# Half of a second expert layer computed token-major instead of feature-major, with the orders of GpSimd and VectorE changed around it

## The chip, the cores and the metric

One core of a Trainium2 chip. The metric is the device time of one execution in microseconds (us); a kernel's time is the median over its runs.

## The reference

1024 tokens with 256 features go through two residual blocks. Block 1 is a gated unit whose weights are the context `ctx[e]` (4 experts of 256 x 256) for gate, up and down alike; each token has one expert, given by its id. Block 2 is a mixture of 16 experts of width 96, top 4 of a sigmoid router, and a shared expert.

```python
def block1(x, ids):                     # h = layernorm(x)
    e = minimum(clip(ids, 0, 12499) // 3125, 3)     # the token's expert
    z = h @ ctx[e].T
    return x + (silu(z) * z) @ ctx[e].T             # x1
def block2(x1):                         # h = layernorm(x1)
    s = sigmoid(h @ router.T)
    w = top4(s + bias) weights of s, normalised to sum 1
    routed = sum_e w[e] * (silu(h @ gate[e].T) * (h @ up[e].T)) @ down[e].T
    return x1 + routed + shared(h)
```

## The kernel before

Tokens are two halves of 512. Activations are feature-major: 128 features on the partitions, the tokens of a half along the free axis, two such chunks (KC) for 256 features. Every fp32 product is made of three fp32r matmuls (high x high, low x high, high x low), so each operand is split into a high part (ScalarE, sometimes VectorE) and a low part (GpSimd for weights, VectorE for activations). The five engines have each its own program, written out by hand in order, and meet at semaphores.

**Block 1.** A `mix(n)` is one output chunk of one layer and half, for all four experts: `mixes` numbers them (layer, half, chunk). Each expert has a PSUM bank of a ring of six (`ring_order`, `ring_bank`); `wait_ring_read` makes TensorE wait until the former contents of a bank are read. ScalarE copies expert 0 (`first_z`, semaphore `z_first`), VectorE overwrites it with experts 1 to 3 where the token's id is beyond a threshold (`pick`, `copy_predicated`, semaphore `z_picked`). For layer 1 follow silu (`silu_z`), `hidden_product`, `hidden_high` or `hidden_cast`, `hidden_low` (semaphore `h1_done`). For layer 2 `add_block_1` adds the residual `xt`, which is x feature-major and becomes x1 in place.

**The norm of block 2.** It needs token-major tiles. For half 0 TensorE transposes x1 (`x1_transposes`, line 1010) into two PSUM banks during mix 5; VectorE takes the statistics there (`tile_stats`, L670; `layer_norm_vars`, L676 and L678), GpSimd the power -0.5 (`rstd_of`, L478), VectorE and ScalarE normalise two tiles each (L721, L542), and TensorE turns the tiles back (`norm_transposes`, L987) for the high and low parts xn_hi, xn_lo (`x_high`, `x_low`; semaphores `xhi_done`, `xlo_done`). Half 1 goes through DRAM instead (`turn_x1`, `write_x1`, `read_x1`, `turn_xn`, `write_xn`, `read_xn`), during the items of block 2.

**Block 2.** Item g is a pair (half, chunk of 128 hidden columns); chunk 0 is the shared expert with the router's logits. `gate_or_up(g)` are the products, `product`, `hidden_2`, `hid_high` and `hid_low` make the hidden chunk, `down(g)` follows two items later. The router's part of VectorE is `turn_logits` (L796, L800), `mark_best` (L807 to L816) and `normalise_scores` (L821 to L833); the combine rows go to DRAM and come back spread over partitions (`write_rows`, `spread_rows`) on the queue of SyncE (SP). `output(h)` adds `xt`.

**Weights.** 15 pieces are loaded by SP into four stage slots in order, `load_piece(n)` waiting for the high and the low part of piece n-4 (`w_hi`, `w_lo`). `high_part` is ScalarE's, `low_part` GpSimd's (L468 in one call, L472 in two calls of 512). Pieces 0 to 3 are ctx, 4 the shared expert and router, 5 and 8, 9, ... gate and up, 6 the shared down weights, 7, 10, 13 the down weights.

## Time and profile before

| | us |
|---|---|
| median of 3 runs (169.2 to 170.2) | 169.52 |
| the profiled execution | 169.34 |
| its span, first to last instruction | 167.2 |
| TensorE busy | 162.5 |
| VectorE / ScalarE / GpSimd busy | 114.5 / 68.7 / 37.2 |

The profile is of one execution. PE is TensorE's matmuls, PEld its weight loads, DVE VectorE, ACT ScalarE, POOL GpSimd, SPq the issues on SyncE's queue. Times in the trace are microseconds from the span's start. L1030 is line 1030 of the kernel before.

### The profile page before, as it was taken

Reading aid. Unit: us, or ns where it says so; the run is one execution under the profiler, and the core shown is the slowest. Engines: PE = TensorE matmul, PEld = TensorE weight load, DVE = VectorE, ACT = ScalarE, POOL = GpSimd, SP = SyncE. Lnnn points to the kernel's source line nnn. Section 1 sums busy time; section 2 is a strip of 40 time slices with the busy share of each in tenths; the row PEclk is TensorE's granted clock in tenths of the full one; section 3 lists DMA queues with packets and bytes.
Section 4 is the critical chain, followed back from the end, with each engine's and each line's share of the span. In section 5 each row is a group of like instructions: output and inputs, shape, how many; then the busy total and the mean of one; then the engine's idle time right before and its main releaser. Section 6 shows DMA issues by size and latency. Waiting matters only on the chain.

```text
span 167.2 us, 2186 instructions
## 1 busy us (share of the span) xinstructions
PE 162.5 (97%) x705; PEld 128.9 (77%) x705; DVE 114.5 (68%) x237; ACT 68.7 (41%) x116; POOL 37.2 (22%) x36
## 2 busy tenths in 40 slices
PE   7999999999999999999999999999999999999992
PEld 2788888888778888888888878888888888888880
DVE  1889999666957998779986744967714444444462
ACT  3654342831359134536734538452222222222210
POOL 1384000656241045556970000000000000000000
PEclk9999999999999999999999999999999999999999
DMA  5891380164304065987225400025441112200003
GB/s 172 275 408 44 107 291 0 21 206 161 115 4 127 16 205 192 219 240 211 67 61 163 153 0 4 1 103 165 173 141 67 63 63 63 65 0 0 4 0 125
DMA packets 12199, 18.78 MB, mean 112 GB/s; under 512 B 3772, under 2 KB 6044, under 8 KB 12060
## 3 DMA queue, kind: packets, MB, share of 16 engines
q1 hardware_dynamic: 12188, 18.64, 34.9%
q8 instruction: 6, 0.10, 0.2%
q14 instruction: 5, 0.04, 0.1%
HBM read 16.39 MB, written 2.24 MB: 111 GB/s over the span
## 4 chain that ended last, share of the span: by engine, by line
PE 95%; DMA 2%; DVE 1%; DVEq 0%; issue 0%
PE bank L1030 23%; PE bank L1131 15%; PE bank L1129 13%; PE bank L1130 13%; PE bank L1149 7%; PE bank L1152 7%; PE bank L1150 7%; DMA first<-first_d 2%; PE bank L998 1%; PE bank L1071 1%; PE bank L1065 1%; PE bank L1126 1%; PE bank L1125 1%; PE bank L987 1%; PE bank L1078 1%; PE bank L1060 1%
## 5 line engine op out<-in xcount | busy, mean ns | idle before, releaser
L1131 PE MATMUL bank<-xn_lo,gu_hi 128*128 128x512 f32 (+1 forms) x104 | 41.1, 395 | 0.0
L1129 PE MATMUL bank<-xn_hi,gu_lo 128*128 128x512 f32 x96 | 38.0, 396 | 0.0
L1130 PE MATMUL bank<-xn_hi,gu_hi 128*128 128x512 f32 x96 | 38.0, 396 | 0.0
L599 ACT ACTIVATE h_hi<-hid 128x512 fp32r<-128x512 f32 (+1 forms) x26 | 16.4, 632 | 45.6 <-DVE hid L860 45.6
L865 DVE TENSOR_TENSOR h_lo<-hid,h_hi 128x512 fp32r<-128x512 f32 (+1 forms) x26 | 18.0, 691 | 14.9 <-ACT h_hi L599 14.9
L1131 PEld LDWEIGHTS bank<-xn_lo,gu_hi 128*128 128x128 f32 (+1 forms) x104 | 19.4, 187 | 4.9
L589 ACT ACTIVATE act_sb<-bank 128x512 f32<-128x512 f32 (+1 forms) x26 | 15.4, 592 | 17.5 <-PE bank L1131 17.4
L472 POOL TENSOR_TENSOR gu_lo<-stage,gu_hi 128x512 fp32r<-128x512 f32 x12 | 17.2, 1457 | 21.7 <-ACT gu_hi L504 16.3
L1129 PEld LDWEIGHTS bank<-xn_hi,gu_lo 128*128 128x128 f32 x96 | 18.0, 188 | 4.4
L1130 PEld LDWEIGHTS bank<-xn_hi,gu_hi 128*128 128x128 f32 x96 | 18.0, 188 | 4.3
L749 DVE COPY_PREDICATED prod<-beyond,bank 128x512 f32<-128x512 uint8 x24 | 17.6, 737 | 5.1 <-PE bank L1030 4.4
L1149 PE MATMUL bank<-h_hi,wd_lo 128*128 128x512 f32 (+1 forms) x52 | 20.6, 396 | 0.0
L1150 PE MATMUL bank<-h_hi,wd_hi 128*128 128x512 f32 (+1 forms) x52 | 20.6, 395 | 0.0
L1152 PE MATMUL bank<-h_lo,wd_hi 128*128 128x512 f32 (+1 forms) x52 | 20.5, 395 | 0.0
L860 DVE TENSOR_TENSOR hid<-prod,bank 128x512 f32<-128x512 f32 x24 | 16.5, 688 | 2.0
L847 DVE TENSOR_TENSOR prod<-act_sb,ids 128x512 f32<-128x512 f32 x12 | 9.6, 796 | 8.6 <-ACT act_sb L589 8.6
L847 DVE TENSOR_TENSOR prod<-act_sb,first 128x512 f32<-128x512 f32 x12 | 10.0, 832 | 6.3 <-ACT act_sb L589 5.7
L1030 PE MATMUL bank<-h_hi,ctx_hi 128*128 128x512 f32 x32 | 12.7, 398 | 0.0
L1030 PE MATMUL bank<-h_lo,ctx_hi 128*128 128x512 f32 x32 | 12.7, 395 | 0.0
L1030 PE MATMUL bank<-h_hi,ctx_lo 128*128 128x512 f32 x32 | 12.7, 395 | 0.0
L1152 PEld LDWEIGHTS bank<-h_lo,wd_hi 128*128 128x128 f32 (+1 forms) x52 | 9.8, 188 | 2.4
L1150 PEld LDWEIGHTS bank<-h_hi,wd_hi 128*128 128x128 f32 (+1 forms) x52 | 9.8, 188 | 2.3
(102 smaller groups left out, 213.2 us busy)
## 6 DMA issues: line engine op xcount, KB each, us to landing
stage<-gu_d SPq DMA_DIRECT2D x6, 512.0 KB, 3.9
stage<-wd_d SPq DMA_DIRECT2D x3, 512.0 KB, 4.3
first<-comb_d SPq DMA_DIRECT2D x8, 192.0 KB, 2.9
ids<-comb_d SPq DMA_DIRECT2D x8, 192.0 KB, 3.3
stage<-ctx_d SPq DMA_DIRECT2D x4, 256.0 KB, 6.0
xt<-xt_d SPq DMA_DIRECT2D x1, 1024.0 KB, 9.9
first<-comb_d SPq DMA_DIRECT2D x8, 128.0 KB, 3.0
ids<-comb_d SPq DMA_DIRECT2D x8, 128.0 KB, 2.9
```

The source lines that it names most:

```text
L472: ins = nc.gpsimd.tensor_tensor(lo[:, s], st[:, s], hi[:, s].bitcast(F32), ALU.subtract)
L749: nc.vector.copy_predicated(prod[:, n % 2], beyond[:, e - 1, h * HALF:(h + 1) * HALF], ring_bank("z", n, e)[:]).then_inc(z_picked, 1)
L847: nc.vector.tensor_tensor(prod[:, g % 2], act_sb[:, g % 2], rows, ALU.mult).then_inc(prod_done, 1)
L860: nc.vector.tensor_tensor(hid[0:w, g % 2], src, up_bank(g)[0:w, :], ALU.mult).then_inc(hid_done, 1)
L865: nc.vector.tensor_tensor(h_lo[0:w, slot[g]], hid[0:w, g % 2], h_hi[0:w, slot[g]].bitcast(F32), ALU.subtract).then_inc(hlo_done, 1)
L1030: return nc.tensor.matmul(ring_bank("z", n, e)[:], (ctx_hi, ctx_lo)[a][:, m, e, k], parts[k][b], start=start, stop=stop)
L1129: nc.tensor.matmul(out[:], gu_lo[:, cols], xn_hi[:, h, k], start=(k == 0), stop=False)
L1130: nc.tensor.matmul(out[:], gu_hi[:, cols], xn_hi[:, h, k], start=False, stop=False)
L1131: ins = nc.tensor.matmul(out[0:rows, :], gu_hi[:, wide], xn_lo[:, h, k], start=False, stop=(k == KC - 1))
L1149: nc.tensor.matmul(acc[k][:], wd_lo[0:w, c, cols], hi, start=(c == 0), stop=False)
L1150: nc.tensor.matmul(acc[k][:], wd_hi[0:w, c, cols], hi, start=False, stop=False)
L1152: ins = nc.tensor.matmul(acc[k][:], wd_hi[0:w, c, cols], lo, start=False, stop=(c == ITEMS - 1))
```

## The change

Layer 2 of block 1 for half 0 is computed token-major by `row_mix`: a tile of 128 tokens of the hidden state is the stationary operand, and the columns of two experts (2 x 256) are the moving one, so a bank holds two experts for one tile. ScalarE copies expert 0 (`row_z`), VectorE picks experts 1 to 3 with a mask per partition (`pick_rows`) and adds x (`add_rows`); x1 is then token-major in `x1_rows`, where the statistics and the normalisation read it. The transposes of x1 of half 0 go. The tokens of a tile are permuted (`hidden`), and the turn of the normalised tiles undoes this. The output of half 0 still needs x1 feature-major: VectorE turns it in blocks of 32 (`turn_x0`, items 8 and 9) and it goes through DRAM (`write_x0`, `read_x0`, items 12 and 13) into `xt`. `xt` of half 0 holds x token-major until then, loaded by a DMA of its own; the ids come a second time, one per partition and tile.

Mix (1, 1, 1) now comes after `row_mix`, so there are 6 mixes. GpSimd takes `rstd_of(0)` ahead of piece 2 and `rstd_of(1)` ahead of piece 3; `rstd_of(2)` and the wait for xn_lo of half 0 come ahead of pieces 6 and 7 (before, behind them). VectorE does all picks of mix 3 ahead of `layer_norm_apply(2)`; before, the statistics came between the first pick and the other two of that mix.

```diff
...
-        ring_order = [("z", n, e) for n in range(7) for e in range(E1)]
-        ring_order += [("gate", 0, 0), ("up", 0, 0)] + [("z", 7, e) for e in range(E1)]
+            count = (HALVES * KC if what == "n2" else 0) + h * KC + k + 1
+            eng.wait_ge(xhi_done, max(count, KC))
+            eng.wait_ge(xlo_done, count)
+
+        ring_order = [("z", n, e) for n in range(3) for e in range(E1)]
+        ring_order += [("rows", t, pair) for t in range(TT) for pair in range(2)]
+        ring_order += [("z", n, e) for n in (3, 4) for e in range(E1)]
...
+            elif what == "rows" and e == 0:
+                eng.wait_ge(row_first, n + 1)
+                eng.wait_ge(row_picked, n * (E1 - 1) + 1)
+            elif what == "rows":
+                eng.wait_ge(row_picked, (n + 1) * (E1 - 1))
         def side_bank(what, h, c):
...
+        def hidden(tile, b, at):
+
+            if b >= KC:
+                return tile[:, at]
+            order = "p (b t j) -> p b t j" if tile is hid else "p (t b j) -> p b t j"
+            return tile[:, at].rearrange(order, t=TT, j=LANES)
         def widths(c):
...
-            sp.dma_start(xt[:], xt_d).then_inc(xt_in, 16)
+            sp.dma_start(xt[:, :, HALF:], xt_d[:, :, HALF:]).then_inc(xt_in, 16)
+            sp.dma_start(id_rows[:], id_rows_d).then_inc(id_rows_in, 16)
+            sp.dma_start(xt[:, :, 0:HALF], x_rows_d).then_inc(x_rows_in, 16)
             sp.dma_start(bias[:], bias_d.partition_broadcast(P)).then_inc(bias_in, 16)
...
+
+            def write_x0():
+                sp.wait_ge(x0_turned, TT)
+                rows = turn_d.rearrange("q k i (b c) -> b i (q k) c", c=P)
+                blocks = x[:, TT:].rearrange("p t d -> p (t d)").rearrange("p (m c) -> p m c", c=P)
+                for b in range(QUARTERS):
+                    sp.dma_start(rows[b], blocks[b * LANES:(b + 1) * LANES]).then_inc(x0_out, 16)
+
+            def read_x0():
+                sp.wait_ge(x0_out, QUARTERS * 16)
+                rows = turn_d.rearrange("q k i n -> q i k n")
+                for q in range(QUARTERS):
+                    sp.dma_start(xt[q * LANES:(q + 1) * LANES, :, 0:HALF], rows[q]).then_inc(x0_back, 16)
...
             pool.wait_ge(deviation_zero, 1)
-            for n in range(E1):
+            low_part(0)
+            low_part(1)
+            rstd_of(0)
+            low_part(2)
+            rstd_of(1)
+            low_part(3)
+            for n in range(E1, E1 + 2):
                 low_part(n)
-            rstd_of(0)
-            rstd_of(1)
-            for n in range(E1, E1 + 3):
-                low_part(n)
-            pool.wait_ge(x1_done, KC)
-            low_part(E1 + 3)
             rstd_of(2)
             pool.wait_ge(xlo_done, (HALVES + 1) * KC)
-            for n in range(E1 + 4, early_pieces + 4):
+            for n in range(E1 + 2, early_pieces + 4):
                 low_part(n)
             rstd_of(3)
...
             first_z(2)
-            first_z(3)
+            row_z(0)
             silu_z(2)
             hidden_high(2)
+            row_z(1)
             high_part(4)
             high_part(5)
+            row_z(2)
             high_part(6)
-            first_z(4)
+            row_z(3)
             high_part(7)
             high_part(8)
             router_low_rows()
-            first_z(5)
-            silu_z(5)
+            first_z(3)
+            silu_z(3)
             apply_norm(2)
             x_high("n2", 0, 0)
             x_high("n2", 0, 1)
-            first_z(6)
+            first_z(4)
             router_logits(0)
             score(0)
             silu_gate(0)
-            first_z(7)
+            first_z(5)
             hid_high(0)
             late_pieces = {1: 9, 2: 10, 3: 11, 5: 12, 6: 13, 7: 14}
...
+
+            def pick_rows(t, experts=range(1, E1)):
+
+                dve.wait_ge(row_first, t + 1)
+                dve.wait_ge(rows_masked, E1 - 1)
+                for e in experts:
+                    dve.wait_ge(row_done, 2 * t + e // 2 + 1)
+                    if e > 1:
+                        dve.wait_ge(row_picked, t * (E1 - 1) + e - 1)
+                    z = ring_bank("rows", t, e // 2)[:, e % 2 * D:(e % 2 + 1) * D]
+                    nc.vector.copy_predicated(x1_rows[:, t], beyond_rows[:, e - 1, t:t + 1].to_broadcast([P, D]),
+                                              z).then_inc(row_picked, 1)
+
+            def add_rows(t):
+
+                dve.wait_ge(row_picked, (t + 1) * (E1 - 1))
+                dve.wait_ge(x_rows_in, 16)
+                residual = xt[:, t * D // HALF, t * D % HALF:][:, 0:D]
+                nc.vector.tensor_tensor(x1_rows[:, t], x1_rows[:, t], residual, ALU.add).then_inc(row_added, 1)
+
+            def turn_x0(first):
+
+                dve.wait_ge(xn_out, QUARTERS * 16)
+                blocks = x[:, TT:].rearrange("p t d -> p (t d)").rearrange("p (q k t i) -> p t k q i", k=KC, t=TT, i=LANES)
+                for t in range(first, first + 2):
+                    for k in range(KC):
+                        ins = nc.vector.transpose(blocks[:, t, k],
+                                                  x1_rows[:, t, k * P:(k + 1) * P].rearrange("p (q i) -> p q i", i=LANES))
+                    ins.then_inc(x0_turned, 1)
+
             def hidden_product(n):
...
             masked.append(thresholds(1))
+            row_thresholds()
             pick(2, masked[1])
-            pick(3, masked[0], [1])
+            pick_rows(0, [1])
             hidden_product(2)
-            pick(3, masked[0], [2])
+            pick_rows(0, [2])
             hidden_low(2)
-            pick(3, masked[0], [3])
-            add_block_1(3)
-            pick(4, masked[0])
+            pick_rows(0, [3])
+            add_rows(0)
+            for t in range(1, TT):
+                tile_stats(2, t - 1)
+                pick_rows(t)
+                add_rows(t)
+            tile_stats(2, TT - 1)
+            layer_norm_vars(2)
+            pick(3, masked[1])
+            layer_norm_apply(2)
+            hidden_product(3)
+            hidden_cast(3)
+            hidden_low(3)
+            x_low("n2", 0, 0)
+            x_low("n2", 0, 1)
+            pick(4, masked[1], [1])
+            turn_logits(0)
+            pick(4, masked[1], [2])
+            normalise_scores(0, mark_best(0))
+            pick(4, masked[1], [3])
             add_block_1(4)
             pick(5, masked[1], [1])
-            for t in range(TT):
-                tile_stats(2, t)
-            layer_norm_vars(2)
+            hidden_2(0)
             pick(5, masked[1], [2, 3])
-            layer_norm_apply(2)
-            hidden_product(5)
-            hidden_cast(5)
-            hidden_low(5)
-            x_low("n2", 0, 0)
-            x_low("n2", 0, 1)
-            pick(6, masked[1], [1])
-            turn_logits(0)
-            pick(6, masked[1], [2])
-            normalise_scores(0, mark_best(0))
-            pick(6, masked[1], [3])
-            add_block_1(6)
-            pick(7, masked[1], [1])
-            hidden_2(0)
-            pick(7, masked[1], [2, 3])
-            add_block_1(7)
+            add_block_1(5)
             hid_low(0)
             for g in range(1, N):
...
-                ins.then_inc(side_done, 1)
+            def row_mix():
+
+                hi, lo = ([w[:, b].rearrange("p (t c) -> p t c", c=P) for b in range(KC)] for w in (h_hi, h_lo))
+
+                def moving(w, pair, k):
+                    return w[:, :, 2 * pair:2 * pair + 2, k].rearrange("p m e f -> p e m f")
+
+                for t in range(TT):
+                    for pair in range(2):
+                        wait_ring_read(pe, "rows", t, pair)
+                        out = ring_bank("rows", t, pair)[:].rearrange("p (e m f) -> p e m f", e=2, m=KC)
+                        for k in range(KC):
+                            if t == 0 and pair == 0:
+                                pe.wait_ge(h1_high, k + 1)
+                            nc.tensor.matmul(out, hi[k][:, t], moving(ctx_hi, pair, k), start=(k == 0), stop=False)
+                            nc.tensor.matmul(out, hi[k][:, t], moving(ctx_lo, pair, k), start=False, stop=False)
+                            if t == 0 and pair == 0:
+                                pe.wait_ge(h1_done, k + 1)
+                            ins = nc.tensor.matmul(out, lo[k][:, t], moving(ctx_hi, pair, k), start=False, stop=(k == KC - 1))
+                        ins.then_inc(row_done, 1)
             def mix(n, between={}, experts=range(E1), features=range(KC)):
...
             first_mix()
             mix(1, {1: lambda: norm_transposes("n1", 1, 1)})
-            for n in range(2, 5):
-                mix(n)
-            mix(5, {1: lambda: (x1_transposes(0, 0), x1_transposes(0, 1))})
-            mix(6, features=[0])
+            mix(2)
+            row_mix()
+            mix(3)
+            mix(4, features=[0])
             norm_transposes("n2", 2, 0)
-            mix(6, experts=[0, 1], features=[1])
+            mix(4, experts=[0, 1], features=[1])
             gate_or_up(0, False)
             gate_or_up(0, True)
-            mix(6, experts=[2, 3], features=[1])
-            mix(7)
+            mix(4, experts=[2, 3], features=[1])
+            mix(5)
             for g in range(1, N):
                 gate_or_up(g, False)
```

## Rows read from the trace of the kernel before

**Rows 1.** The page: busy time by engine, PE's busy slices, the chain.

```profile
PE 162.5 (97%) x705; PEld 128.9 (77%) x705; DVE 114.5 (68%) x237; ACT 68.7 (41%) x116; POOL 37.2 (22%) x36
...
PE   7999999999999999999999999999999999999992
...
PE 95%; DMA 2%; DVE 1%; DVEq 0%; issue 0%
```

**Rows 2.** The chain in order of time: start, duration, what.

```profile
39.06 0.87 PE bank L1010 x8
```

**Rows 3.** Timeline of VectorE, 14 to 47 us: start, duration, instruction, idle before.

```profile
14.67 0.73 DVE L721 TENSOR_SCALAR xn<-first,meanvar,rstd 128x256 f32<-128x256 f32 x2
...
28.69 0.69 DVE L757 TENSOR_TENSOR hid<-act_sb,prod 128x512 f32<-128x512 f32 x1
...
39.83 1.41 DVE L670 BATCH_NORM_STATS2 stats<-bank 128x6 f32<-128x256 f32 x4
...
42.77 0.74 DVE L749 COPY_PREDICATED prod<-beyond,bank 128x512 f32<-128x512 uint8 x1 [0.16 <-PE bank L1030]
...
43.46 0.99 DVE L721 TENSOR_SCALAR xn<-bank,meanvar,rstd 128x256 f32<-128x256 f32 x2
...
45.55 0.69 DVE L769 TENSOR_TENSOR h_lo<-hid,h_hi 128x512 fp32r<-128x512 f32 x1
```

**Rows 4.** Timeline of TensorE, 46 to 57 us.

```profile
46.72 0.39 PE L1030 MATMUL bank<-h_lo,ctx_hi 128*128 128x512 f32 x1
...
56.01 0.40 PE L1030 MATMUL bank<-h_hi,ctx_hi 128*128 128x512 f32 x1
```

**Rows 5.** Timeline of GpSimd, 34 to 64 us.

```profile
34.79 0.74 POOL L468 TENSOR_TENSOR wd_lo<-stage,wd_hi 96x256 fp32r<-96x256 f32 x1
37.91 2.54 POOL L472 TENSOR_TENSOR wd_lo<-stage,wd_hi 128x512 fp32r<-128x512 f32 x2 [2.38 <-DVE xt L777]
41.94 1.01 POOL L478 TENSOR_TENSOR rstd<-vareps,power 128x4 f32<-128x4 f32 x1 [1.49 <-DVE vareps L678]
48.33 2.55 POOL L472 TENSOR_TENSOR gu_lo<-stage,gu_hi 128x512 fp32r<-128x512 f32 x2 [5.38 <-DVE xn_lo L728]
60.63 2.99 POOL L472 TENSOR_TENSOR gu_lo<-stage,gu_hi 128x512 fp32r<-128x512 f32 x2 [9.75 <-ACT gu_hi L504]
```

**Rows 6.** Timeline of VectorE, 50 to 56 us: logits, top-4, picks.

```profile
50.73 0.24 DVE L800 TENSOR_TENSOR logit<-turned 128x64 f32<-128x64 f32 x1
51.48 0.74 DVE L749 COPY_PREDICATED prod<-beyond,bank 128x512 f32<-128x512 uint8 x1 [0.51 <-PE bank L1030]
52.11 0.21 DVE L807 TENSOR_TENSOR biased<-scores,bias 128x64 f32<-128x64 f32 x1
52.35 0.41 DVE L811 MAX8 best<-biased 128x8 f32<-128x16 f32 x4
...
53.66 0.23 DVE L821 SCALAR_TENSOR_TENSOR weight<-marked,scores 128x64 f32<-128x64 f32 x1
...
55.09 0.70 DVE L749 COPY_PREDICATED prod<-beyond,bank 128x512 f32<-128x512 uint8 x1
```

**Rows 7.** Timeline of VectorE where GpSimd is or isn't at work.

```profile
9.46 0.65 DVE L678 TENSOR_SCALAR vareps<-meanvar 128x4 f32<-128x4 f32 x1
...
12.50 0.17 DVE L678 TENSOR_SCALAR vareps<-meanvar 128x4 f32<-128x4 f32 x1
...
60.86 1.61 DVE L847 TENSOR_TENSOR prod<-act_sb,first 128x512 f32<-128x512 f32 x1 [0.18 <-DMA first<-comb_d]
```

**Rows 8.** Timeline of GpSimd and TensorE, 8 to 14 us.

```profile
8.79 3.80 POOL L468 TENSOR_TENSOR ctx_lo<-stage,ctx_hi 128x512 fp32r<-128x512 f32 x3 [1.01 <-ACT ctx_hi L504]
12.55 1.18 POOL L478 TENSOR_TENSOR deviation<-vareps,power 128x4 f32<-128x4 f32 x1
...
12.84 0.40 PE L1030 MATMUL bank<-xn_hi,ctx_hi 128*128 128x512 f32 x1
```

**Rows 9.** Timeline of VectorE and TensorE, 94 to 99 us.

```profile
94.66 1.28 DVE L728 TENSOR_TENSOR xn_lo<-xn,xn_hi 128x512 fp32r<-128x512 f32 x2
...
98.46 0.40 PE L1131 MATMUL bank<-xn_lo,gu_hi 128*128 128x512 f32 x1
```

More of the change, by code:

```diff
@@ L62 @@
 XN_TURN, XN_WRITE, XN_READ = 6, 10, 11
+X0_TURN, X0_WRITE, X0_READ = 8, 12, 13
 SPREADS = 4
@@ L201, in wait_side_read @@
             what, h, k, _ = before[-1]
-            if what in ("n1", "n2"):
-                count = (HALVES * KC if what == "n2" else 0) + h * KC + k + 1
-                eng.wait_ge(xhi_done, max(count, KC))
-                eng.wait_ge(xlo_done, count)
-            else:
-                eng.wait_ge(normed_v, (HALVES + 1) * TT // 2)
-                eng.wait_ge(normed_a, (HALVES + 1) * TT // 2)
-        ring_order = [("z", n, e) for n in range(7) for e in range(E1)]
-        ring_order += [("gate", 0, 0), ("up", 0, 0)] + [("z", 7, e) for e in range(E1)]
+            count = (HALVES * KC if what == "n2" else 0) + h * KC + k + 1
[4 more added lines that the diff above has]
+        ring_order += [("z", n, e) for n in (3, 4) for e in range(E1)]
+        ring_order += [("gate", 0, 0), ("up", 0, 0)] + [("z", 5, e) for e in range(E1)]
         ring_at = {u: n for n, u in enumerate(ring_order)}
@@ L296, in wait_mixed @@
             layer, h, m = mixes[n]
-            eng.wait_ge(h1_done if layer == 1 else x1_done, h * KC + m + 1)
+            if layer == 1:
+                eng.wait_ge(h1_done, h * KC + m + 1)
+            else:
+                eng.wait_ge(x1_done, m + 1)
         downs = [place[h, c] for h in range(HALVES) for c in range(ITEMS)]
@@ L450, in _ @@
                     read_xn()
+                if g == X0_WRITE:
+                    write_x0()
+                if g == X0_READ:
+                    read_x0()
                 if g == place[1, SPREADS]:
@@ L523, in first_z, with row_z @@
                 nc.scalar.activation(prod[:, n % 2], ring_bank("z", n, 0)[:], ACT.Copy).then_inc(z_first, 1)
+            def row_z(t):
+                act.wait_ge(row_done, 2 * t + 1)
+                nc.scalar.activation(x1_rows[:, t], ring_bank("rows", t, 0)[:, 0:D], ACT.Copy).then_inc(row_first, 1)
             def centre(t):
@@ L546, in hidden_high @@
                 act.wait_ge(h1_product, b + 1)
-                nc.scalar.activation(h_hi[:, b], hid[:, b % 2], ACT.Copy).then_inc(h1_high, 1)
+                nc.scalar.activation(hidden(h_hi, b, b), hidden(hid, b, b % 2), ACT.Copy).then_inc(h1_high, 1)
             def router_low_rows():
@@ L750, in pick, with row_thresholds @@
                                               ring_bank("z", n, e)[:]).then_inc(z_picked, 1)
+            def row_thresholds():
+                dve.wait_ge(id_rows_in, 16)
+                for e in range(1, E1):
+                    nc.vector.tensor_scalar(beyond_rows[:, e - 1], id_rows[:], float(e * PER_EXPERT), None,
+                                            ALU.is_ge).then_inc(rows_masked, 1)
+            def pick_rows(t, experts=range(1, E1)):
[21 more added lines that the diff above has]
+                    ins.then_inc(x0_turned, 1)
             def hidden_product(n):
@@ L762, in hidden_cast @@
                 dve.wait_ge(h1_product, b + 1)
-                nc.vector.tensor_scalar(h_hi[:, b], hid[:, b % 2], 1.0, None, ALU.mult).then_inc(h1_high, 1)
+                nc.vector.tensor_scalar(hidden(h_hi, b, b), hidden(hid, b, b % 2), 1.0, None, ALU.mult).then_inc(h1_high, 1)
             def hidden_low(n):
@@ L768, in hidden_low @@
                 dve.wait_ge(h1_high, b + 1)
-                nc.vector.tensor_tensor(h_lo[:, b], hid[:, b % 2], h_hi[:, b].bitcast(F32),
+                nc.vector.tensor_tensor(hidden(h_lo, b, b), hidden(hid, b, b % 2), hidden(h_hi, b, b).bitcast(F32),
                                         ALU.subtract).then_inc(h1_done, 1)
```

51 lines of the change are left out of this document (30 added, 21 removed).

## The prediction

> **What bounds the kernel now.** I read the page first. TensorE (PE) is busy for 97% of the span, and the chain that ended last is 95% PE [rows 1]; its busy row stands at 9 tenths or more in every slice but the first and the last [rows 1]. So the time is the length of PE's own program plus the moments in which it waits, and between those two slices it waits nowhere. An edit can help only by what it takes off PE, and hurts as soon as another engine comes later than PE's next need. The second view is therefore the timeline of PE around the edit, and the third those of VectorE (DVE) and GpSimd (POOL), to find how long ahead of PE each product is ready.
>
> **What it takes off PE.** The second layer of half 0 keeps its arithmetic: two `mix` calls of 4 experts x 2 chunks x 3 products are 48 matmuls of 512 columns; `row_mix` has 4 tiles x 2 expert pairs x 2 chunks x 3 = 48 of 512 columns too. Only the stationary and the moving side change places. Eight transposes of x1 go, and the chain has them as one piece of 0.87 us [rows 2]. PE starts a 512-column matmul each 0.233 us (162.5 us of busy time for 705, a few of them small [rows 1]), so 0.87 us is everything that the edit can give: 0.51% of the span. The moving side is now four runs of 128 elements with gaps, and no row shows such a read; I take it at nothing, as the transposes and half-width matmuls go at the pace of their columns. The other bound would be half speed, 48 x 0.233 = 11 us slower; nothing in the trace speaks for it.
>
> **The row picks (31 to 44 us).** Two copies, six picks and two adds of 512 columns become four copies (ScalarE), twelve picks and four adds of 256. A 512-wide pick takes 0.74 us [rows 3]. A 256-wide operation on PSUM takes 0.50 (the two normalisations take 0.99) and 0.35 to 0.41 per statistics call (1.41 for four) [rows 3]; so a pick lies between 0.37 (half) and 0.74 (no saving), and I take 0.47. A tile then costs DVE 3 x 0.47 + 0.42 for the add + 0.37 for the statistics = 2.2 us, and PE delivers a tile each 12 x 0.233 = 2.8 us. DVE starts behind, since half 1's hidden product comes between. The last pick of mix 2 ends some 0.7 before the hidden product, which starts at 28.69 [rows 3]; with three new 128x4 thresholds I put it at 28.2. From there DVE has 12 picks 5.6, 4 adds 1.7, 4 statistics 1.5, product and low part 1.4, aggregation and epsilon 0.6, then three 512-wide picks of mix 3 at 0.75 = 2.25: 13.0 us, plus about 0.6 waiting for ScalarE: 41.8. The third pick can't start before PE has finished mix 3: it started at 42.77, so 41.9 now, and would end at 42.65, against 43.51 before [rows 3]: hidden. But each add reads two SBUF tensors, and POOL's low parts of pieces 4 and 5, which follow ScalarE's high parts behind the hidden product, run then; as below, an add that meets one waits for it. Two such waits of 0.7 to 0.9 put the end at 43.4. What still hides that: the two vector normalisations read SBUF now (0.73 a pair at 14.67, instead of 0.99), and the low part of the hidden product ends at 46.24 before, while PE's third matmul of the next group, which reads it, starts at 46.72 [rows 3, 4]. Limit for the pick's end: (46.72 - 0.87) - (46.24 - 43.51 - 0.26) = 43.38. So 0 to 0.2 us are lost here. With picks at 0.74 it would be 12 x 0.27 = 3.2 more.
>
> **The two weight pieces (46 to 56 us), the decisive part.** Before, POOL has done pieces 6 and 7 by 40.45, and after half 0's xn_lo it has only piece 8, two calls, 48.33 to 50.88, with DVE's logits and top-4 behind it [rows 5, 6]. Now rstd_of(2) goes first and pieces 6, 7 and 8 all follow xlo_done: from 48.33 - 0.87 = 47.46, 0.74 for piece 6 and twice 2.55: to 53.3 at least [rows 5]. That gains nothing where it is meant to, since the norm waits for DVE's third pick (42.65), not for the power (1.0 us from about 41.2, so 42.3 [rows 5]). And it collides. When DVE has an operation whose operands lie in SBUF while POOL works, it waits for the end of POOL's call: the epsilon add took 0.65 us at 9.46, ending with POOL's second ctx piece, and 0.17 at 12.50; the product at 60.86 took 1.61 instead of 0.69, with POOL's pair at 60.63 stretched to 2.99 [rows 5, 7, 8]. Statistics and picks from PSUM show no such growth.
> Times, all shifted by 0.87. The logit sum (50.73 before) comes at 49.86, inside piece 7's second call (49.47 to 50.73), and ends near 50.9. The third mix's pick then runs to 51.6 and the bias add (52.11 before, 51.24 shifted) meets piece 8's first call (50.9 to 52.15): the top-4 chain begins at 52.4 instead of 51.48 [rows 6]. That is 0.92 late. Its max and match calls have one SBUF tensor and should pass; the next with two, the weight product (53.66 before, 53.7 now), comes just when piece 8's second call ends (52.35 to 53.6). So rows and the last pick are 0.92 late: the pick ends at 55.79 - 0.87 + 0.92 = 55.84. PE needs just that pick: expert 3 of the last mix overwrites the bank that it reads. Before, it ended at 55.79 and PE's matmul started at 56.01 [rows 4, 6]; now PE is there at 55.14. It waits until about 55.9: 0.77 us lost. A loss upstream isn't added, since POOL's start doesn't move with it.
> The Trainium skill, in "SBUF — State Buffer", section "SBUF: two separate sides", says that a DVE operation with two SBUF inputs or in a two-port mode and a GpSimd operation hold one port pair in turn, each for the whole instruction. The trace agrees (0.65 against 0.17, 1.61 against 0.69). By it the match calls, with a single SBUF input, are free.
>
> **The first 25 us.** The power for half 0 now comes ahead of ctx piece 2 and that for half 1 ahead of piece 3. Piece 1 ends at 10.06; 1.0 to 1.2 for the power and 1.27 for piece 2 give 12.5, and mix 1 starts at 12.84 [rows 8]: 0.3 of cover. Piece 3 ends at 15.0 and makes the shift and the normalisations of half 1 0.3 late; its PE consumers stand 0.05 to 0.5 behind. The deviations turn after the thresholds either way. I take 0, bounds 0 and +0.3.
>
> **Transfers and the way back.** xt becomes two loads of half the size and a third of 2 KB for the ids, issued in the first microseconds and needed from 31 us; hidden, though the small rstd rows queue behind them as they do now. SP's load of piece 12 waits for piece 8's low part (53.6) and stands ahead of the combine rows, which come just before the last pick (55.1): no cost. At g = 8 and 9 DVE gets 8 block transposes of 128x128, about 0.3 each, 1.2 per item. The second set delays half 1's xn_lo from 94.66 to about 96.4; its first piece (0.65) is done at 97.1 and PE reads it at 98.46 [rows 9]: 1.3 us spare. The four writes hold SP until x0 is turned, then spread rows and read back are done by 103, and `output(0)` comes at 117. All 0.
>
> **Sum.** Profiled execution 169.34 (span 167.2 + 2.1). 169.34 - 0.87 + 0.77 = 169.24, that is -0.1; on the median of 169.52 it is 169.4. A difference of 0.5%, 0.85 us, is about what a measurement can tell.
>
> **Rivals.** (a) *Full gain*, 168.65 to 169.0: the logit sum or the bias add slips between two POOL calls. For it: 0.3 us of misalignment decides each. Against: POOL works without a gap from 47.5 to 53.5. Chance 0.22; only its lowest third is over 0.5% faster. (b) *Slower*: the top-4 chain is held a second time, by piece 8's second call, because the match calls need the port after all or because the weight product comes before 53.6. Price: another 1.27, on the median 169.52 - 0.87 + 0.77 + 1.27 = 170.7. It decides when POOL's last call ends later than 53.7 and holds DVE for over 0.95. For it: the margin of 0.1. Against: the statistics calls pass freely. Chance 0.13. (c) *Row chain late*: picks near 0.74 put 1 to 3 us before PE at 45 us: 169.5 + 0.3 to 172. Chance 0.08, half of it over 0.5%. (d) The forecast, 169.1 to 169.8: 0.57.
>
> Range 168.6 (nothing lost) to 170.5. Faster by over 0.5%: 0.08; within: 0.76; slower: 0.16.
>
> **What the profile after would show.** 697 matmul records instead of 705; no transposes of xt; `row_mix` with 48 matmuls at 0.233 without a gap; picks of 256 at 0.4 to 0.5; POOL busy from 47.5 to 53.5; the logit sum and the bias add at 0.8 and 0.6 us instead of 0.24 and 0.21; one PE gap of some 0.7 us before the last mix's fourth expert, released by DVE's pick. No gap there is (a); a match or weight call of over 1 us is (b); a PE gap near 45 us is (c). Wrong altogether if `row_mix` matmuls last longer than 0.40.

## The result, and the profile after

The kernel became slower. Six executions of it take 171.43 us in the median (171.19 to 171.91), six of the kernel before on the same chip 169.86 (169.2 to 170.2); the ratio is 1.0112, with an interval of 1.0095 to 1.013. The forecast was 169.4 and its range ended at 170.5. The profiled execution took 171.42 us with a span of 169.3, where the one before took 169.34 with 167.2.

The page of the kernel after, the lines that answer to [rows 1]:

```profile
PE 161.9 (96%) x697; PEld 127.3 (75%) x697; DVE 122.0 (72%) x256; ACT 69.1 (41%) x118; POOL 37.0 (22%) x36
...
PE   7799999999999599999999999999999999999992
...
PEclk9999999999999999999999999999999999999999
...
PE 88%; DVE 3%; DMA 3%; issue 2%; ACT 1%; POOL 1%; SPq 0%; DVEq 0%; POOLq 0%
```

TensorE has 0.6 us less to do and eight matmuls fewer, as it should. But one slice in the middle, the fourteenth, falls to 5 tenths, and the second is down from 9 to 7. The view of TensorE's waits names what ended each (columns: us in total, times, longest). The wait of 1.2 us stands in the kernel before too; the two last are for the first `ctx` pieces:

```profile
PE bank L1132 <- DVE prod L798: 1.9, 1, 1.9
PE bank L1067 <- DVE warm L961: 1.2, 1, 1.2
PE bank L1180 <- ACT ctx_hi L541: 0.9, 1, 0.9
PE bank L1167 <- POOL ctx_lo L505: 0.2, 1, 0.2
```

The first is the wait for VectorE's pick before the last mix's expert 3, the very one that the prediction named. The timeline of TensorE shows its size; it answers to [rows 4]:

```profile
55.71 0.40 PE L1132 MATMUL bank<-h_lo,ctx_hi 128*128 128x512 f32 x1
57.99 0.49 PE L1132 MATMUL bank<-h_hi,ctx_hi 128*128 128x512 f32 x1 [1.89 <-DVE prod L798]
```

From start to start that is 2.28 us, where 0.23 is the pace: 2.05 lost. The timelines of VectorE and GpSimd show why, against [rows 6] and [rows 5]. VectorE:

```profile
50.60 3.15 DVE L885 TENSOR_TENSOR logit<-turned 128x64 f32<-128x64 f32 x1
53.66 0.72 DVE L798 COPY_PREDICATED prod<-beyond,bank 128x512 f32<-128x512 uint8 x1
54.29 0.20 DVE L892 TENSOR_TENSOR biased<-scores,bias 128x64 f32<-128x64 f32 x1
...
57.26 0.68 DVE L798 COPY_PREDICATED prod<-beyond,bank 128x512 f32<-128x512 uint8 x1
```

GpSimd:

```profile
47.92 0.74 POOL L505 TENSOR_TENSOR wd_lo<-stage,wd_hi 96x256 fp32r<-96x256 f32 x1 [5.36 <-DVE xn_lo L777]
48.62 2.54 POOL L509 TENSOR_TENSOR wd_lo<-stage,wd_hi 128x512 fp32r<-128x512 f32 x2
51.11 2.55 POOL L509 TENSOR_TENSOR gu_lo<-stage,gu_hi 128x512 fp32r<-128x512 f32 x2
```

The logit sum, 0.24 us of work, took 3.15. It reached VectorE at 50.60, half a microsecond before piece 7's second call ended, and did not run when that ended at about 51.1, nor at the boundary at about 52.4, but only when GpSimd's whole run was over at 53.66. Everything behind it, the last pick at 57.26 instead of 55.09 before, is 2.2 us late.

The whole difference of 2.1 us in span adds up by the first starts of the stages of TensorE. Before and after, with what each stage adds in brackets, they are: half 0's second layer 24.90 and 25.35 (+0.45), the transposes of the norm behind it 45.37 and 44.94 (-0.88, the removed transposes), the gate of half 0 47.64 and 47.51 (+0.30), expert 3 of the last mix 56.01 and 57.99 (+2.11, the gap of 2.05 and its surroundings). The +0.45 comes with the waits for the first `ctx` pieces in the list above, which vary by the execution (see experiment 1). Without it +1.6 would be left, which is also the difference of the medians. That agreement is in part chance: the profiled execution before is 0.5 us under its median, and whether the other executions after have the +0.45 isn't known.

### The profile page after: what moved, and what is told of

It reads as the page before. It is cut to its first block, busy times and chain, and to the rows that moved or that the text cites. A ratio compares the mean times of both kernels' runs of the same rounds, so it can differ in the third digit from the quotient of the medians.

```text
span 169.3 us, 2206 instructions
## 1 busy us (share of the span) xinstructions
PE 161.9 (96%) x697; PEld 127.3 (75%) x697; DVE 122.0 (72%) x256; ACT 69.1 (41%) x118; POOL 37.0 (22%) x36
## 4 chain that ended last, share of the span: by engine, by line
PE 88%; DVE 3%; DMA 3%; issue 2%; ACT 1%; POOL 1%; SPq 0%; DVEq 0%; POOLq 0%
PE bank L1233 14%; PE bank L1132 14%; PE bank L1232 13%; PE bank L1231 13%; PE bank L1251 7%; PE bank L1254 7%; PE bank L1252 7%; DMA stage<-ctx_d 3%; PE bank L1109 2%; PE bank L1113 2%; PE bank L1110 2%; PE bank L1167 1%; PE bank L1173 1%; PE bank L1080 1%; DVE prod L798 1%
## 5 line engine op out<-in xcount | busy, mean ns | idle before, releaser
L798 DVE COPY_PREDICATED prod<-beyond,bank 128x512 f32<-128x512 uint8 x18 | 13.1, 735 | 0.6
L1251 PEld LDWEIGHTS bank<-h_hi,wd_lo 128*128 128x128 f32 (+1 forms) x52 | 9.8, 188 | 2.4
L1132 PE MATMUL bank<-xn_hi,ctx_hi 128*128 128x512 f32 x24 | 9.6, 399 | 0.0
L1132 PE MATMUL bank<-xn_lo,ctx_hi 128*128 128x512 f32 x24 | 9.5, 395 | 0.0
```

The costliest lines, as they stand in the source:

```text
L1132: return nc.tensor.matmul(ring_bank("z", n, e)[:], (ctx_hi, ctx_lo)[a][:, m, e, k], parts[k][b], start=start, stop=stop)
L1251: nc.tensor.matmul(acc[k][:], wd_lo[0:w, c, cols], hi, start=(c == 0), stop=False)
```

## The experiments

Each kernel ran beside the kernel before on the same chip; that one's median was 169.3 to 169.6 in all of them. "Run" below means a row of GpSimd calls that follow one another at once.

**1. Undo one part: the two weight pieces stay ahead of the power.**

```diff
-            for n in range(E1, E1 + 2):
+            for n in range(E1, E1 + 4):
                 low_part(n)
             rstd_of(2)
             pool.wait_ge(xlo_done, (HALVES + 1) * KC)
-            for n in range(E1 + 2, early_pieces + 4):
+            for n in range(E1 + 4, early_pieces + 4):
```

> The changed kernel with GpSimd's low parts of pieces 6 and 7 back ahead of rstd_of(2). Theory A (the logit sum is held by GpSimd's unbroken run over pieces 6, 7 and 8, 50.60 to 53.75): the sum takes 0.25 us again, the PE gap of 2.1 us before the last mix's fourth expert is gone, and the time is that of before minus 0.87 plus what is lost elsewhere (0.45 early, 0.3 at the hidden low part at most): 168.9 to 169.8, ratio to before 0.995 to 1.000. Rival B (the row picks and the new waits make VectorE late whatever GpSimd does): it stays at 171.4, ratio 1.01.

Measured: 169.15 us (168.73 to 170.23, 12 executions), ratio 0.9982 (0.9963 to 1.0002). The gap in the last mix is gone. The timeline of VectorE at the logits:

```profile
50.79 0.23 DVE L885 TENSOR_TENSOR logit<-turned 128x64 f32<-128x64 f32 x1
```

So the moved pieces cost the time, and the rest of the change gives at most a few tenths.

Where the +0.45 of the kernel after comes from is only in part clear. ScalarE's first high part of `ctx` started at 5.75 us before, 6.40 after, and 5.72 to 5.97 in all experiments but 15. Experiments 11, 14 and 15 profile one kernel three times: the high part starts at 5.75, 5.72 and 6.84, the second layer at 24.69, 24.86 and 25.80, and only the last has waits for `ctx` (0.8 and 0.2). So a late `ctx` is of the execution and can cost 1 us. But this experiment has `ctx` on time (5.88) and its second layer starts at 25.22, little ahead of 25.35; how much of the +0.45 the late `ctx` made isn't shown.

Of the 0.87, then, 0.32 is lost here by the start of the second layer, and 0.62 between the norm's transposes and the gate, which are 2.89 us apart (2.27 before):

```profile
44.81 1.36 PE L1080 MATMUL bank<-first,xn 128*128 128x128 f32 x8
...
47.70 0.39 PE L1227 MATMUL bank<-xn_hi,gu_hi 128*128 128x512 f32 x1
```

There VectorE is the late one: from 14 us on it pauses only twice, for 0.37 and 0.34 us at 29 and 31 us, both times for ScalarE. Part of its lateness is the row adds, which meet pieces 4 to 7:

```profile
31.83 1.13 DVE L825 TENSOR_TENSOR x_rows<-x_rows,xt 128x256 f32<-128x256 f32 x1
...
34.91 0.72 DVE L825 TENSOR_TENSOR x_rows<-x_rows,xt 128x256 f32<-128x256 f32 x1
...
37.60 0.62 DVE L825 TENSOR_TENSOR x_rows<-x_rows,xt 128x256 f32<-128x256 f32 x1
...
40.17 0.43 DVE L825 TENSOR_TENSOR x_rows<-x_rows,xt 128x256 f32<-128x256 f32 x1
```

**2. Do that part alone: the kernel before with pieces 6 and 7 moved behind `xlo_done`, nothing else.**

```diff
-            for n in range(E1, E1 + 3):
-                low_part(n)
-            pool.wait_ge(x1_done, KC)
-            low_part(E1 + 3)
+            for n in range(E1, E1 + 2):
+                low_part(n)
             rstd_of(2)
             pool.wait_ge(xlo_done, (HALVES + 1) * KC)
-            for n in range(E1 + 4, early_pieces + 4):
+            for n in range(E1 + 2, early_pieces + 4):
```

> The kernel before with only GpSimd's order of pieces 6 and 7 changed: behind rstd_of(2) and the wait for xn_lo. Theory A: the logit sum waits from 50.7 to the end of piece 8 at about 54.2, and PE waits some 2.4 us before expert 3 of mix 7: 172.0 to 172.5, ratio 1.013 to 1.016. Rival B: no change, 169.9, ratio 1.00.

Measured: 173.39 us (171.79 to 174.21, 6), ratio 1.0207 (1.0164 to 1.0249). The logit sum starts at 50.98, is held to the end of the run at 54.34, and TensorE's gap is the same:

```profile
50.98 3.44 DVE L798 TENSOR_TENSOR logit<-turned 128x64 f32<-128x64 f32 x1
54.34 0.72 DVE L747 COPY_PREDICATED prod<-beyond,bank 128x512 f32<-128x512 uint8 x1
```

So the part alone does it, and costs more than the 2.4 us that were expected. The rest stands in the windows of this kernel (columns: busy time and count by engine, granted clock, share of DMA, GB/s):

```profile
56.00:60.00 4.00, 2.10 (x10) 1.40 (x9) 3.69 (x17) 1.09 (x3) 0.00 (x0) 0.99 0.34 129
60.00:64.00 4.00, 4.00 (x12) 3.17 (x11) 3.29 (x7) 1.47 (x3) 0.00 (x0) 0.58 0.45 126
64.00:68.00 4.00, 4.00 (x19) 3.20 (x18) 3.22 (x4) 2.86 (x4) 2.84 (x3) 1.00 0.42 138
```

Behind the gap the granted clock is 0.58 of full speed for some 4 us, thus mostly at 1.2 GHz instead of 2.4: 12 matmuls in the window, where the next has 19. Seven of 0.233 us are 1.6 us. The kernel after has the same gap and no such fall:

```profile
60.00:64.00 4.00, 4.00 (x19) 3.22 (x18) 3.69 (x5) 2.16 (x3) 1.29 (x2) 1.00 0.46 160
```

It goes by the execution: in experiment 2 the two with a mean clock of 1.0 took 171.79 and 172.06, the four at 0.99 took 173.31 to 174.21. At full clock the price is thus 2.3 to 2.6, as expected.

**3. Keep the order and put a pause into the run: GpSimd waits for the logit sum ahead of piece 8.**

```diff
             for n in range(E1 + 2, early_pieces + 4):
+                if n == E1 + 4:
+                    pool.wait_ge(logit_summed, 1)
                 low_part(n)
```

> The changed kernel with one wait more: GpSimd starts piece 8 only when the logit sum is done. Theory A with the sum passed over between two calls of GpSimd that follow at once: the sum ends with piece 7, at 51.2, instead of 53.75. The bias add then meets piece 8's first call: if it gets in between the two calls, the PE gap falls from 2.1 to about 1.0 us (170.3, ratio 1.003 to 1.006); if it is passed over as well, to 1.6 (171.0). Rival C (the sum isn't held by GpSimd's calls but by something between it and ScalarE, as the table load beside it): no change, 171.4.

Measured: 169.34 us (169.14 to 169.88, 12), ratio 0.9994 (0.9979 to 1.0008). VectorE, then GpSimd:

```profile
50.23 0.65 DVE L887 TENSOR_TENSOR logit<-turned 128x64 f32<-128x64 f32 x1
...
51.62 0.71 DVE L894 TENSOR_TENSOR biased<-scores,bias 128x64 f32<-128x64 f32 x1
52.37 0.41 DVE L898 MAX8 best<-biased 128x8 f32<-128x16 f32 x4
...
53.67 0.23 DVE L908 SCALAR_TENSOR_TENSOR weight<-marked,scores 128x64 f32<-128x64 f32 x1
```

```profile
48.24 2.54 POOL L509 TENSOR_TENSOR wd_lo<-stage,wd_hi 128x512 fp32r<-128x512 f32 x2
50.95 2.55 POOL L509 TENSOR_TENSOR gu_lo<-stage,gu_hi 128x512 fp32r<-128x512 f32 x2 [0.16 <-DVE logit L887]
```

That is the picture the prediction drew: the sum waits for piece 7's second call alone, the bias add for piece 8's first call, max and match run freely beside the second, and the weight product misses it. So it is GpSimd's calls that hold the sum (rival C is out), and the result is better than theory A's 170.3, because TensorE loses only 0.34 at the last pick. With 0.16 us of pause the kernel stands 1.2% better against the kernel before than with none (0.9994 for 1.0112).

**4. The early power order alone: the powers of half 0 and 1 behind the four `ctx` pieces, as before.**

```diff
-            low_part(0)
-            low_part(1)
-            rstd_of(0)
-            low_part(2)
-            rstd_of(1)
-            low_part(3)
+            for n in range(E1):
+                low_part(n)
+            rstd_of(0)
+            rstd_of(1)
```

> The changed kernel with the powers of the two first norms behind all four ctx pieces again, as before. Theory A: the early order costs or gives nothing on PE: 171.2 to 171.6, as the changed kernel. Rival D (the 0.45 us that PE is late at 13 us come from this order): 171.0, and mix 1 starts at 12.8 instead of 13.3.

Measured: 172.42 us (170.99 to 172.84, 6), ratio 1.0149 (1.0111 to 1.0187). The sum is held as in the kernel after (50.49, 3.14 us) and the gap is the same. Two executions at full clock took 170.99 and 171.15, four at 0.99 took 172.41 to 172.84 (0.67 in 60 to 64 us of the profiled one). At full clock that is 1.6 us above its own kernel before, as the kernel after is (1.57): the order of the powers makes no difference here, and the higher median is the clock's.

**5 and 6. Why is the sum passed over? Smaller calls, and the run shifted.** Experiment 5 cuts pieces 7 and 8 into four calls of 256 columns each. Experiment 6 puts one more power (1.0 us) ahead of piece 6, so that the sum meets another place of the run.

```diff
-                for part in range(2):
+                parts = 4 if n in (E1 + 3, E1 + 4) else 2
+                for part in range(parts):
...
```

> The changed kernel with the low parts of pieces 7 and 8 in four calls of 256 columns each (0.65 us or so) instead of two of 512. Theory A1 (VectorE's request is served only at some boundary, by its phase against GpSimd's calls): the logit sum gets in at one of the six boundaries after 50.6 and takes 0.3 to 1.5 us. Theory A2 (this sum, once it waits, is passed over for as long as calls follow at once): it still ends when piece 8 ends, at about 53.8 to 54.5, however small the calls.

```diff
...
             pool.wait_ge(xlo_done, (HALVES + 1) * KC)
+            nc.gpsimd.tensor_tensor(spare[:], power[:], power[:], ALU.pow)
             for n in range(E1 + 2, early_pieces + 4):
```

> The changed kernel with one power of 128x4 more on GpSimd ahead of piece 6 (1.0 us, into a spare tile), so that its run comes a microsecond later against VectorE's program. Theory A1 (phase): the logit sum at 50.6 now falls into piece 7's first call and gets in behind it, 0.3 to 1.2 us. Theory A2: it is held to the end of the run, about 54.7, and the PE gap grows by 1 us to 3.1 (span 170.3).

Measured, one execution each: 169.51 us and 171.1 us. With small calls the sum gets in at a boundary inside the run, though GpSimd has no pause:

```profile
50.40 0.30 DVE L886 TENSOR_TENSOR logit<-turned 128x64 f32<-128x64 f32 x1
...
51.78 0.31 DVE L893 TENSOR_TENSOR biased<-scores,bias 128x64 f32<-128x64 f32 x1
...
53.43 0.73 DVE L907 SCALAR_TENSOR_TENSOR weight<-marked,scores 128x64 f32<-128x64 f32 x1
```

The weight product is held by the last call here, which is rival (b)'s second hold at 0.5 us. With the run shifted, the sum is held for 4.08 us, over three boundaries. So experiment 5 goes by theory A1 and experiment 6 by A2: neither decides alone, and it isn't a matter of the one phase of the kernel after. The time of experiment 6 can't be set beside the others. Its matmuls start 0.227 us apart (30.05, 30.27, 30.50, 30.73), in every other profile 0.233, at a granted clock of 1.00 in both; over some 660 matmuls of 512 columns that is, as an estimate, 4 us. It hides a first gap of 1.0 us, the one of 2.05 and the fall of the clock behind it.

**7. Is it this instruction? Another small addition, `turned` and `bias` into a spare tile, ahead of the sum.**

```diff
                 dve.wait_ge(dstep, steps[0])
+                if h == 0:
+                    dve.wait_ge(bias_in, 16)
+                    nc.vector.tensor_tensor(spare[:], turned[:, :, 0:E2], bias[:].unsqueeze(1).to_broadcast([P, TT, E2]), ALU.add)
```

> The changed kernel with one more addition of VectorE ahead of the logit sum of half 0: the turned logits plus the bias row, 128x64, into a spare tile, two SBUF tensors of which only one is the turned logits. Theory S (the logit sum is special, both its inputs lie in one tile): the new addition gets in at the next boundary between GpSimd's calls (51.15) and takes 0.3 to 0.9 us; the sum behind it is held to the end of the run, 53.7. Theory R (whichever small operation waits there is passed over by calls that follow at once): the new addition is held to the end of the run, about 3 us, and the sum behind it takes 0.25.

Measured, one execution: 171.99 us.

```profile
50.98 3.13 DVE L886 TENSOR_TENSOR spare<-turned,bias 128x64 f32<-128x64 f32 x1
54.04 0.21 DVE L889 TENSOR_TENSOR logit<-turned 128x64 f32<-128x64 f32 x1
```

The other addition is held in its place and the sum is free behind it: the hold belongs to the moment, not to the sum's operands.

**8 and 9. Win back what experiment 1 loses: pieces out of the adds' way.** Both have the pieces ahead of the power, as in experiment 1, and hold pieces 4, 5 and 6 until VectorE has done row adds 1, 2 and 3; experiment 9 has the late powers of experiment 4 too.

```diff
             for n in range(E1, E1 + 4):
+                if n < E1 + 3:
+                    pool.wait_ge(row_added, n - E1 + 1)
                 low_part(n)
```

> The changed kernel with pieces 6 and 7 ahead of rstd_of(2) again, and pieces 4, 5 and 6 each started only when VectorE's add of tile 0, 1 and 2 is done. Theory E (what is left of the loss in the version with the pieces back is VectorE's program from 30 to 46 us, stretched by the adds that wait for GpSimd, 0.7 and 0.3 us): the adds take 0.42 each but perhaps the fourth, the norm's turn and the hidden low part come 0.6 to 1.0 us earlier, and the time is 168.6 to 168.9, ratio 0.995 to 0.997. Rival F (the remaining loss lies before 25 us only): as the version with the pieces back, 169.15, ratio 0.998.

> As the run before it, with the two first powers behind all four ctx pieces as in the kernel before. Theory E2 (the order of the powers makes VectorE's shift of half 1 wait for ctx piece 3, 0.75 instead of 0.15 us, and with it everything to 30 us): the shift takes 0.15, the hidden low parts of half 0 come 0.3 to 0.5 earlier, PE has no gap at 15.5, and the time is 168.4 to 168.7, ratio 0.993 to 0.996. Rival G (the early order is neutral or helps): equal to or slower than the run before it.

Measured: 169.68 us (169.16 to 171.63, 12), ratio 1.002 (0.9996 to 1.0044), and 169.41 (168.96 to 170.64, 12), ratio 1.001 (0.9992 to 1.0028). Neither reaches what was expected. The first two adds are free (0.43), but the pieces, now later, meet the others (0.95 and 1.65), the fourth one across a boundary. The powers' order is worth 0.27 between the two medians, less than their intervals.

**10 and 11. Smaller calls from piece 4 on.** Pieces ahead of the power as in experiment 1, and every GpSimd call of the weights cut to 256 columns or half a piece; experiment 11 with the late powers too.

```diff
-                if pieces[n][2] < STAGE:
+                cols = pieces[n][2]
+                if n < E1:
...
-                for part in range(2):
-                    s = slice(part * STAGE // 2, (part + 1) * STAGE // 2)
+                parts = 4 if cols == STAGE else 2
+                for part in range(parts):
+                    s = slice(part * cols // parts, (part + 1) * cols // parts)
```

> The changed kernel with pieces 6 and 7 ahead of rstd_of(2) and GpSimd's calls from piece 4 on cut to 256 columns (224 and 128 in the short pieces), about 0.72 us each, so that a VectorE operation that meets one waits for at most 0.7 instead of 1.3 us. Theory E (the remaining loss against the gain of 0.87 is VectorE's program of 15 to 46 us, stretched by waits for whole calls): the four adds take 0.4 to 0.8 each, VectorE is 0.3 to 0.7 earlier at the norm and PE's loss there falls from 0.6 to 0.0 to 0.3: 168.6 to 168.9, ratio 0.995 to 0.997. Rival F (more calls mean more meetings and a longer run of GpSimd, 2.86 instead of 2.54 a piece): 169.1 to 169.5, ratio 0.998 to 1.000.

> As the run before it with the two first powers behind the four ctx pieces, as in the kernel before. Theory E2: VectorE's shift of half 1 takes 0.15 instead of 0.75 and PE's gap at 15.5 us is under 0.1: another 0.2 to 0.4 us, 168.4 to 168.7, ratio 0.993 to 0.996. Rival G (it is neutral): as the run before it.

Measured for experiment 10: six executions, 168.02 and 168.53, and four of 170.72 to 170.85. For experiment 11: 168.44 us in the median of 12, eight of 168.05 to 168.89 and four of 170.53 to 170.97. Its ratio, 0.9957 (0.9924 to 0.999), leaves two of the four long ones out. The profiled execution is a short one, span 166.2, and keeps the 0.87 whole: its norm transposes start at 44.29, the gate at 46.62, 1.02 us ahead of before. With experiment 13 below it is the best version that was found, but its time has two values 2.3 us apart.

**12 to 15. What makes the long executions?** Experiment 12 keeps the small calls to pieces 4 to 8 (the theory: many small calls later in the program). Experiment 13 adds experiment 3's wait ahead of piece 8 to experiment 11 (the theory: the logit sum is passed over in some executions). Experiments 14 and 15 are two more profiles of experiment 11's kernel.

```diff
-                parts = 4 if cols == STAGE else 2
+                parts = (4 if n < early_pieces else 2) if cols == STAGE else 2
```

> As the run with small calls and late powers, with the small calls for pieces 4 to 8 only; from piece 9 on GpSimd has two calls of 512 again, as before and after the change. In that run 4 of 12 executions took 170.5 to 171.0 instead of 168.0 to 168.9. Theory L (a small call later on, in the items of block 2, holds VectorE's product or norm in some executions): no execution is over 169.3, median 168.4 to 168.6. Rival M (the 2.3 us are lost at the logit sum behind piece 8, at 50 us, where the calls are still small): again about a third of the executions at 170.5 to 171.0.

> The version with pieces back, small calls and late powers, with one wait more: GpSimd starts piece 8 only when the logit sum is done. Theory M (in the long executions of that version the logit sum is passed over by piece 8's calls): no execution is over 169.3, median 168.1 to 168.5, ratio 0.991 to 0.995. Rival N (another operation is, among the adds and the epsilon of 30 to 41 us): again about a third of the executions at 170.5 to 171.0.

> A second look at the version with pieces back, small calls and late powers, the kernel unchanged. A span of 166.2 shows nothing new; one of 168.7 shows where the 2.3 us are: by theory M a logit sum of 2 us or more, by rival N an add or the epsilon, by a third way (the data of a weight piece or the combine rows come late) a wait on a DMA.

> As the look before it: a span of 166.2 shows nothing new, one of 168.7 shows which operation or transfer is late.

Measured: experiment 12 has 169.14 us (12 executions, four of them 170.75 to 171.11), ratio 1.0019 (0.9984 to 1.0053): the later calls aren't it. Experiment 13 has 168.94 us (8, two of them 170.84 and 171.07), ratio 0.9949 (0.9927 to 0.9971, one of the two left out): the logit sum isn't it either. Its profiled execution is a long one, and shows it. VectorE, then GpSimd:

```profile
37.15 2.55 DVE L827 TENSOR_TENSOR x_rows<-x_rows,xt 128x256 f32<-128x256 f32 x1
```

```profile
31.32 4.46 POOL L511 TENSOR_TENSOR gu_lo<-stage,gu_hi 128x224 fp32r<-128x224 f32 x6 [16.54 <-ACT gu_hi L543]
35.75 3.67 POOL L511 TENSOR_TENSOR wd_lo<-stage,wd_hi 96x128 fp32r<-96x128 f32 x6
```

The third row add is passed over by three boundaries of small calls, until the run ends at 39.42. VectorE is without a pause there, so that the 1.8 us by which this add is longer than in a short execution reach TensorE at the norm; they are most of the 2.3. Experiment 14 (170.52 us) is long as well, with the add at 36.97 and 2.56. Experiment 15 (169.29, with the late `ctx`) isn't:

```profile
37.45 0.78 DVE L825 TENSOR_TENSOR x_rows<-x_rows,xt 128x256 f32<-128x256 f32 x1
```

```profile
36.04 0.89 POOL L511 TENSOR_TENSOR wd_lo<-stage,wd_hi 96x128 fp32r<-96x128 f32 x2
37.20 3.01 POOL L511 TENSOR_TENSOR wd_lo<-stage,wd_hi 128x256 fp32r<-128x256 f32 x4 [0.27 <-ACT wd_hi L541]
```

GpSimd had to wait 0.27 us for ScalarE's high part of piece 7, and the add got in behind the first call after that pause. The short profiled executions of experiments 10 and 11 have the same pause (0.27 and 0.28); that of experiment 12, also short, shows none, so a pause isn't needed.

The long and the short also differ earlier. From the start of the second layer to the first row add it is 6.13 to 6.27 us in the four short profiles (experiments 10, 11, 12, 15), but 6.80 and 6.60 in the two long ones (13 and 14): VectorE, and GpSimd's run with it, is already 0.3 to 0.7 us further behind TensorE. With the 1.8 that makes the 2.3. That this lateness decides whether the pause comes and the third add is held fits all six, but no experiment moved it alone.

## Why the prediction was wrong

The step that failed is this one: "The logit sum (50.73 before) comes at 49.86, inside piece 7's second call (49.47 to 50.73), and ends near 50.9." The place and the cause were right: the sum does come inside that call, and is held by it; the same pick is late; TensorE waits at the same matmul. What failed is how long one hold can last. I took it from operations which had come inside the first GpSimd call after a pause [rows 5, 7, 8], and concluded that a hold ends with the call. Here it ended with the run, 2.6 us and two boundaries later. The sum is 2.9 us longer than a free one, and the bias add behind it was free, since GpSimd was done. The last pick ended at 57.94, 2.1 us behind the forecast's 55.84; TensorE came there 0.8 later too (55.94 for 55.14: the 0.45 by the start of the second layer and the 0.3 at the norm). The difference, 1.3, is the gap of 2.05 us instead of 0.77. The forecast's sum, -0.87 + 0.77, is in the profile -0.88 + 2.05 + 0.30 + 0.45, or 1.92 of the 2.1.

By its other steps:

- *TensorE's saving of 0.87*: right, 0.88 between the stages. The strided moving side costs nothing: all three products of `row_mix` have a mean of 395 ns, as the others. The reason given for it was partly misread: the transposes don't go at the pace of their columns, for eight of 128 columns fill 0.79 us before (38.90 to 39.69), where 1024 columns of the large matmuls take 0.47.
- *Picks of 256 at 0.47*: measured 0.51 in a run of three (1.54) and 0.43 to 0.45 alone. *Row chain 0 to 0.2*: a size missed by a little, 0.3 lost at the norm, where the adds took 1.14, 0.74, 0.42 and 0.43. With the weight pieces ahead of the power it is 0.62 (experiment 1), so the forecast was near, for an order in which only pieces 4 and 5 stand beside the adds.
- *"The match calls, with a single SBUF input, are free"*: right; in experiment 3 they run beside piece 8 at their usual times. Of the Trainium skill's page "SBUF — State Buffer", section "SBUF: two separate sides", which gives the pair to one instruction for its whole length, the runs bear out that a held operation waits at least to the end of the call that it meets. The hold of 3.15 us over two boundaries doesn't follow from it.
- *First 25 us at 0, bounds 0 and +0.3*: about +0.2 in the mean, with a wide scatter. With `ctx` on time, six profiles with the early powers (experiments 1, 3, 5, 7, 8, 10) start the second layer at 24.87 to 25.61, eight with the late ones (the kernel before, experiments 2, 4, 9, 11 to 14) at 24.69 to 25.16; the means are 25.17 and 24.89. Experiment 6, with its faster matmuls, is left out.
- *Transfers and the way back at 0*: right. Half 1's xn_lo starts at 97.58 instead of 94.66, of which 2.1 us are the whole program's lateness and 0.88 the second set of block transposes, and TensorE has no wait there or after.
- *Rival (b)* had the sign and nearly the size (170.7), but by another mechanism, a second hold by piece 8's second call. The forecast's own picture exists: experiment 3 shows it, with 169.34 us for 169.4. That the total fits so well is luck: 0.34 us is lost at the last pick instead of 0.77, and another 0.42 ahead of the gate, which the forecast put at nothing (the second layer starts 0.03 before that of the kernel before, the gate 0.49 instead of 0.91).
- Not thought of: a gap of 2 us on TensorE can bring the clock down for some 4 us, another 1.5 us (experiments 2, 4 and 6). It didn't in any of the six executions of the kernel after.

What stays open is what lets a waiting VectorE operation in at one boundary and not at another. It got in behind the first call after a pause (experiments 3 and 15), and also inside unbroken runs (experiments 5 and 12, and the second row add of experiment 1, 0.72 us, between the full-size calls of pieces 5 and 6); it was passed over in experiments 2, 4, 6 to 9, 13 and 14. Neither the length of the calls, nor the place in the run, nor the instruction alone decides it, and the same kernel does both from one execution to the next.

## What to carry to other kernels

Where GpSimd runs calls back to back and VectorE must do a small operation on two SBUF tensors that TensorE waits for, count with a hold to the end of the whole run, not of the call; a pause of 0.16 us, made by a wait on that operation's own result, took 1.2% off here. Moving work on an idle engine is free only if nothing on the critical chain is held by it in the new place. And 0.87 us taken off the bounding engine are worth that much only if the next engine has as much to spare: here VectorE had not, and with the collision gone 0.94 of it was lost again in two places in the profiled execution (0.32 and 0.62).

## What the runs showed of the hardware that was not expected

- A VectorE operation of 0.2 us was held over one to three boundaries of GpSimd calls: 3.15 us in the kernel after, 3.44, 3.14, 4.08 and 3.13 in experiments 2, 4, 6 and 7, and 2.55 and 2.56 for a row add that met calls of only some 0.74 us (experiments 13 and 14).
- One program's time can take two values: 168.05 to 168.89 and 170.53 to 170.97 us in experiment 11. The two long executions that were profiled (experiments 13 and 14) have the held add, the four short ones don't.
- After a gap of 2 us on TensorE the granted clock stood at 0.57 to 0.67 in the 4 us from 60 on in some executions and at 1.00 in others; it cost about 1.5 us.
- The first `ctx` piece's high part started between 5.72 and 6.84 us in different executions; where it was latest (experiment 15) the second layer started at 25.80, with the same kernel otherwise at 24.69 and 24.86.
- In the profiled execution of experiment 6 matmuls of 512 columns start 0.227 us apart instead of 0.233, though the granted clock is 1.00 in both. What made this isn't shown.
